# Row maxima first: the order of VectorE's work within an attention slot

## The reference

```python
x = layernorm(x + mamba(x))                        # 512 inner channels, 16 states, 4 taps
x = layernorm(x + attention(latents=x, context))   # 16 heads of 64
x = layernorm(x + experts(x))                      # 8 experts, top 2, and 2 shared ones
# attention, per batch entry:
kv = concat(layernorm(context), layernorm(x)) @ Wkv     # 1601 + 512 = 2113 keys
q = layernorm(x) @ Wq
w = softmax(q @ k.T / 8);  out = (w @ v) @ Wout
```

## Time and profile before

| | us |
|---|---|
| Median of 3 runs | 3040.41 (3039.42 to 3043.43) |
| The profiled execution, its own time | 3045.14 |
| Its span, first to last instruction | 3043.4 |
| PE busy | 2881.4 (95%) |
| DVE busy | 2025.4 (67%) |
| ACT busy | 1638.5 (54%) |
| POOL busy | 1560.1 (51%) |
| Mean granted TensorE clock | 0.981 |

### The profile page before, as it was taken

How to read it: one execution, slowest core, us unless ns; L and a number is a source line. 1 busy time by engine, 2 the same in 40 slices (tenths; PEclk the granted TensorE clock), 3 DMA queues, 4 the chain that set the end, 5 groups by cost and what they waited for, 6 DMA issues and landing times. The chain is left out here.

```text
span 3043.4 us, 36342 instructions
## 1 busy us (share of the span) xinstructions
PE 2881.4 (95%) x12032; PEld 1906.0 (63%) x12032; DVE 2025.4 (67%) x3451; ACT 1638.5 (54%) x2837; POOL 1560.1 (51%) x1235
## 2 busy tenths in 40 slices
PE   7577999999999999999999999999999999899997
PEld 3234565656665656565656565656777777687786
DVE  5897777775658677666687767566555555356666
ACT  5753545453545454535454545366777777525652
POOL 4495757670017575600175756003656667526764
PEclk9898999999999999999999999999999999799999
DMA  6453212111122121211221212110101100421112
GB/s 237 149 180 106 76 36 60 35 53 57 39 70 60 36 66 29 73 37 39 70 67 36 60 36 66 37 39 15 46 20 34 45 17 15 146 74 60 49 46 82
DMA packets 71694, 189.98 MB, mean 62 GB/s; under 512 B 8420, under 2 KB 39272, under 8 KB 63448
## 3 DMA queue, kind: packets, MB, share of 16 engines
q1 hardware_dynamic: 67096, 172.08, 18.7%
q0 software_dynamic: 3984, 15.60, 1.6%
q10 hardware_dynamic: 432, 0.01, 0.0%
HBM read 124.59 MB, written 28.44 MB: 50 GB/s over the span
## 5 line engine op out<-in xcount | busy, mean ns | idle before, releaser
L1148 ACT ACTIVATE a_carry<-a_st 128x512 f32<-128x512 f32 (+1 forms) x1088 | 649.4, 597 | 918.5 <-PE a_st L1590 905.5
L1610 PE MATMUL a_o<-a_carry,a_vals 128*65 128x512 f32 (+1 forms) x1632 | 835.6, 593 | 0.0
L1338 DVE TENSOR_REDUCE a_maxes<-a_mx 128x1 f32<-128x512 f32 x1016 | 677.5, 686 | 189.0 <-PE a_mx L1513 180.9
L964 POOL TENSOR_TENSOR a_plow<-a_carry,a_phigh 128x512 fp32r<-128x512 f32 (+1 forms) x272 | 349.0, 1290 | 259.8 <-ACT a_phigh L1151 256.2
L996 POOL TENSOR_TENSOR a_shared<-a_shared,a_bc 128x512 f32<-128x512 f32 x192 | 250.9, 1307 | 386.7 <-DVE a_shared L1268 386.7
L1590 PE MATMUL a_st<-a_q,a_kone 65*128 65x512 f32 (+1 forms) x1088 | 431.6, 397 | 0.0
L1268 DVE TENSOR_TENSOR_SCAN a_shared<-a_shared 128x512 f32<-128x512 f32 x192 | 290.3, 1514 | 15.9 <-POOL a_shared L983 14.6
L1589 PE MATMUL a_st<-a_q,a_keven 128*128 128x512 f32 (+1 forms) x544 | 295.9, 544 | 2.5 <-ACT a_carry L1148 1.6
L1589 PE MATMUL a_st<-a_q,a_kodd 128*128 128x512 f32 (+1 forms) x544 | 286.8, 527 | 0.0
L1513 PE MATMUL a_mx<-a_kodd,a_q 128*128 128x512 f32 x512 | 275.6, 554 | 10.3 <-DVE a_maxes L1338 9.0
L1590 PEld LDWEIGHTS a_st<-a_q,a_kone 65*128 65x128 f32 (+1 forms) x1088 | 202.0, 186 | 123.6 <-issue 93.2
(11 more groups left out here) (300 smaller groups left out, 5225.3 us busy)
## 6 DMA issues: line engine op xcount, KB each, us to landing
a_bc<-m_kept_bc SPq DMA_DIRECT2D x48, 512.0 KB, 3.7
a_wt<-a_w_split SPq DMA_DIRECT2D x15, 1536.0 KB, 8.6
a_kone<-a_keven SPq DMA_DIRECT2D x32, 528.5 KB, 4.5
a_kone<-a_kodd SPq DMA_DIRECT2D x32, 528.5 KB, 4.2
e_wall<-in_w_t_dram SPq DMA_DIRECT2D x27, 512.0 KB, 5.6
a_shared<-m_kept_bc SPq DMA_DIRECT2D x16, 512.0 KB, 3.9
a_w_split<-a_wt POOLq DMA_DIRECT2D x4, 1536.0 KB, 5.4
a_shared<-in_ctx_dram SPq DMA_DIRECT2D x4, 1536.0 KB
```

The lines of the kernel that those rows point to most:

```text
L964: nc.gpsimd.tensor_tensor(p_low(s)[0:r], p_of(s % 4)[0:r], p_high(s)[0:r].bitcast(F32), ALU.subtract).then_inc(p_low_ready, 1)
L1148: nc.scalar.activation(p_of(s % 4)[0:r], st[0:r, s % 2], ACT.Exp, scale=SCALE).then_inc(exp_done, 1)
L1338: nc.vector.reduce_max(maxes[:, c, t:t + 1], mx_bank(g, i), AX_X).then_inc(mx_max, 1)
L1610: nc.tensor.matmul(ps_o[0:DH + 1, g % 2], vals[0:r, kt * HG + j, :], p_of(s % 4)[0:r], start=(kt == 0), stop=(kt == KT - 1)).then_inc(pv_d ...
```

## The change

In the loop of DVE the list of a slot is sorted: all X (kind `"X"`) come first, the rest after them in the order they had. The other engines' loops are untouched.

```diff
             for g in range(NH):
                 for kt in range(KT):
-                    for what in BESIDE[g][kt]:
+
+                    for what in sorted(BESIDE[g][kt], key=lambda what: what[0] != "X"):
                         make(what)
```

## The result

| | before | after |
|---|---|---|
| Median (lowest to highest) of 4 runs each, same chip, us | 3041.92 (3039.42 to 3044.54) | 3176.3 (3170.94 to 3177.89) |
| Span of the profiled execution, us | 3043.4 | 3176.1 |
| Mean granted clock | 0.981 | 0.975 |

The ratio is 1.0439, interval 1.042 to 1.0457: 134 us slower. The prediction was 3125 with a range up to 3165, so its sign held and its size did not: 49 of the 134 us are missing in it.

A forecast was written before the change was run, and what follows sets the result against it. PE was taken to bound attention: -35 us from fewer waits for maxima and +120 from late evictions and N gave +85, so 3130 on the profiled 3045.1, or 3125 against the median 3040.4; range 3078 to 3165.

The forecast's parts named there:

- V: In 15 heads, O 3 waits for V 1's late copy (24 us) and O 1 for V 0's (31 us).
- Heads 14, 30, 46: T of each slot needs N of the slot before, now late: 14 us a head, 42 us.
- rival A: New waits cost PE its full clock, striking in heads 14, 30 and 46: +88 us, 3213; half, 3169; chance 0.07.
- The sign that I had named for being wrong: One of three such signs: a granted clock under 1.00 anywhere from 600 to 2400 us.
- Slot 8: O 2 waits behind O 0 where slot 6 has a scan: 0.8 us odd heads, 0.4 even, 11 us.
- Slot 6 (14 for 9): First ring product of slot 6 waits for K 3's late low part: about 0.5 us a head, 9 us.
- Term 1, -35: PE's weight loads of X wait less for maxima: -35 us, bounds -29 and -50.
- V 8: V 8 delayed behind V 6 with a scan in slot 0: six heads at 0.5 us, 3 us.
- ACT and POOL at 0: ACT and POOL keep their order and later scans cost them nothing: 0, bounds 0 and some 10 us.
- Rivals B: Later ring evictions stay hidden from PE and the maxima's gain alone is left: 3005 us; chance 0.05.
- C: Delays come to a third (40 us) and cancel the gain: 3040 to 3045 us; chance 0.03.
- D: DVE finds the X ready more often and the delays halve: 3065 to 3080 us; chance 0.10.

The follow-up runs named there:

- v_ahead: Experiment 1: the changed kernel with V copies put ahead of the maxima again, all the rest behind; 3113.17 us.
- experiment 4: Also n_ahead: the changed kernel with each N first in its slot, ahead of the maxima (heads 14, 30 and 46 alone); 3132.17 us.
- experiment 5: Also scans_ahead: the changed kernel with scans put ahead of the maxima again, then the X, then the rest; 3123.49 us.
- o_behind: Experiment 8: the changed kernel, but in slots 7 and 9 of heads with V PE issues O behind `add_o`; 3144.15 us.
- experiment 9: The kernel before, but in slots with a K the low part of K stands last; 3026.32 us.
- t_heads_old: The changed kernel, but heads 14, 30 and 46 keep DVE's old order; 3133.19 us.
- n_ahead: The same run as experiment 4: the changed kernel with each N first in its slot, ahead of the maxima; 3132.17 us.
- v_alone: The kernel before with only the copy of V moved to the end of its slot; 3111.7 us.
- experiment 10: The changed kernel with V copies and scans ahead of the maxima and heads 14, 30 and 46 in the old order; 3030.72 us.
- t_heads_new: The kernel before with the changed order in heads 14, 30 and 46 alone; 3087.94 us.

## Why the prediction was right and wrong

**What bounds, and the mechanism: right.** PE's stream is the bound, and the ring readers came out as the places. The waits for V, N, O and K that the prediction named are the rows above (the one for N had been there, small), and experiments 1, 4, 5, 8 and 9 change them one at a time.

**V: right.** 55 us predicted (the working itself gives 54: 15 x 1.55 is 23.3 and not 24), 54.3 measured without the clock. One wait in slot 9 was put at 1.55 and measured 1.55; one in slot 7 behind a scan at 2.75, and measured 2.79. Experiment 5 takes just the scan's part away: these six heads go to 1.55. Of the fall of slot 7 from 36.8 to 24.8 that is 7.4 us; the rest is clock.

**Heads 14, 30, 46: right.** 14 predicted, 13.5 measured in every head that kept its full clock.

**The first step that failed: the clock has no term in the sum.** "The delays add, since PE is saturated on both sides of each" holds, but they also cost clock, and the sum puts that at nothing. I gave it 0.07, as rival A, looked for it in heads 14, 30 and 46 alone, and argued that in heads with V PE stays busy over 80%. It does, and the clock fell there all the same: head 27's stretch above is 19.35 us long with PE busy 16.73 of it, at 0.91. The sign that I had named for being wrong, a clock under 1.00 from 600 to 2400 us, is there: 0.99. A quarter of rival A came, spread thin: about 21 us, not 88. It followed the longest waits first. Three kernels have the same waits for V (after, t_heads_old, n_ahead): of the six heads with a scan in slot 6, where O 1 waits 2.5 us, five lost clock in after, four in t_heads_old and five in n_ahead; of the other nine heads with V, one, one and none did. With the scans out of the way (experiment 5) none of the six did. The length of the wait does not settle it alone: v_alone, with no wait over 1.7 us, lost clock in nine of the 15. The Trainium skill (TensorE: Matmul & The Clock Gate, section "A second HAM failure mode: psum-queue depth-cycling") says that a kernel which cycles PSUM banks with short pauses can swing between the clock levels; the traces of after and of v_alone agree, with 13 and 12 such falls, none before. What no row here explains is why head 11 kept its clock and head 27, with the same instructions, did not; that cause stays open.

**The second step that failed: what stands behind a late instruction.** I followed a postponed scan to its own slot's evictions, and to the next product. I did not follow it into the next slot, where the next maxima stand behind it. Slots 9 to 11 of head 21, after, DVE:

```profile
1156.31 0.69 DVE L1338 TENSOR_REDUCE a_maxes<-a_mx 128x1 f32<-128x512 f32 x1 [0.33 <-PE a_mx L1514]
1156.92 1.21 DVE L1268 TENSOR_TENSOR_SCAN a_shared<-a_shared 128x512 f32<-128x512 f32 x1
1158.05 0.14 DVE L1350 RECIPROCAL a_rinv<-a_ring 128x1 f32<-128x1 f32 x1
1158.23 0.48 DVE L1352 SCALAR_TENSOR_TENSOR rows<-a_ring,a_rinv,rows 128x256 f32<-128x256 f32 x1
1158.63 1.97 DVE L1338 TENSOR_REDUCE a_maxes<-a_mx 128x1 f32<-128x512 f32 x3
```

and PE:

```profile
1158.14 0.40 PE L1591 MATMUL a_st<-a_q,a_kone 65*128 65x512 f32 x1
1159.37 0.51 PE L1514 MATMUL a_mx<-a_keven,a_q 128*128 128x512 f32 x1 [0.83 <-DVE a_maxes L1338]
```

Slot 9's scan and O push slot 10's maxima to 1158.63, and the X that takes their bank waits 0.83 us. This cost 8.3 us in slot 11. In slot 5 of heads with g%4 = 0, where slot 3 has a scan and V 9, it cost 7.2. Slot 8 came to 15 without the clock, for 11: the odd heads cost the 0.8 each that I had, the even ones 0.3 to 1.4 instead of 0.4. Together 15.5 + 4 = 19.5 us. Experiment 5 shows how much of that is the scans': slot 5 is back at -0.3 and slot 8 at 1.3, but slot 11 keeps 3.1 of its 8.3, in experiment 10 too, where neither scans nor V are late. I take those for O 3 behind slot 9's maximum, which no run tests.

Slot 6 (14 for 9) failed for other reasons. In heads 13, 29 and 45, where J too stands behind the maxima, it grew by 1.2 us instead of 0.5; with K alone late (experiment 9) by 0.24. And 13 heads with no scan in slot 3 grew by 0.2 to 0.5 each, 4 us in all, where I had put nothing.

**Term 1, -35: mis-sized.** The other slots gave -27.6. The wait of the weight loads fell by 34.7 us, but part of a load's wait is the load's normal idle, and where a scan or an O of the slot before is now late, the X finds DVE busy again.

In sum: 21 for the clock, 19.5 for what stands behind a late instruction, 5 for slot 6, 7.4 for the gain, less 2.7 where V, T and V 8 came out under my terms: 50 of the trace's 135, and 49 of the medians' 134. The waits that were left out or put too small weigh somewhat more (24.5) than the clock.

**ACT and POOL at 0: right.** Neither has a row in the waits that grew.

**Rivals B, C and D** fell with the first rows: the ring waits are there, and at full size.

## What to carry to other kernels

In a queue that is worked off strictly in order, as DVE's is in these traces, put first what is ready first; an instruction whose input the producer makes last in a stage belongs at the end of that stage, unless the producer itself is waiting for it. Before moving an instruction back, find who takes its buffer next and how far off that is, and follow what it displaces into the next stage as well. And when a saturated TensorE gets many new waits of over a microsecond, add something for the clock: here 21 us on 114, in the heads of t_heads_new 5 on 40, in v_alone 19 on 57.

## What was not expected of the hardware

- A PE that is busy for 97% of a long stretch (v_alone, 600 to 2400 us) and 86% of a head's slots 6 to 10 (after, head 27) fell to 1.2 GHz for short stretches, after waits of 0.9 to 2.5 us. Each cost 1.2 to 1.6 us. It does not recur from head to head: 11 and 27 hold the same instructions, 17.73 against 19.35 us.
- With V ahead, or with the scans ahead, 3 stretches were left of 14; with both and the T heads back, none. But a count is that of one execution: heads 14, 30 and 46, with the same 24 waits for N, had 8 in after, 4 in t_heads_new, 3 in v_ahead, 2 in scans_ahead and 5 in o_behind. So a part of the fall from 14 to 3 can be chance; no run here tells how large a part.
